# The second expert layer by pairs of experts: blocks of 128 tokens that run both experts and write finished rows

## The chip, the cores and the metric

One core of one Trainium2 chip runs the whole program. The metric is the device time in microseconds of one launch. One execution was also taken with the hardware profiler. Its rows give the traced span, and its own time stands in the table below.

## The reference

The input is 32 sequences of 256 tokens with 128 numbers each, 8192 tokens in all. Four residual blocks follow one another: a gated linear recurrence, a mixture of experts, causal attention with low-rank scores, and the same mixture of experts once more with the same weights. The change is in the last one.

```python
gate_logits = xs @ Wg                                   # 8 experts
weights, sel = jax.lax.top_k(gate_logits, 2)
weights = softmax(weights, axis=1)
h = relu(einsum('td,edf->etf', xs, W1) + b1[:, None, :])   # 128 -> 512
out_e = einsum('etf,efd->etd', h, W2) + b2[:, None, :]     # 512 -> 128
out = einsum('tk,tkd->td', weights, out_e[sel, tok[:, None]])
x = x + out                                             # xs is the layer norm of x
```

## The kernel before

`build` (L2221) calls `scan`, two setups, `ffn` for the first expert layer, `attention` and `ffn` for the second. Each is a block of its own, so the next starts when all engines are done with the last.

**Routing.** `ffn` (L871) loads x, normalises groups of four 128-token tiles (L1252 to L1275), stores the normalised rows to `normed` in DRAM, and computes the logits. VectorE then computes, one operation after another with a wait behind each (`did`, L1295), the two best experts of every token (L1310 to L1320), where each of the 16384 (token, expert) entries stands when they are sorted by expert (L1326 to L1349), and which expert each block of 256 slots belongs to (L1365). The inverse table, slot to token, comes from one-hot matrices: `onehot` (L1352) builds 2 x 128 columns and TensorE sums them (`find`, L1099), in 16 groups of 8.

**The expert loop.** There are 72 blocks (`NB`) of 256 slots, a fixed number, each with one expert. For a block GpSimd fetches 2 x 128 rows by their token number (`fetch`, L1037), TensorE turns them (`turn`), ScalarE and VectorE split them into two halves of 16 bits (`high`, `x_lo`), TensorE runs the first matrix (`up`, 12 matmuls of 256 columns), ScalarE applies bias and relu (L1223), both engines split the result (L1232 and L1410 for the high half, L1414 for the low one), TensorE runs the second matrix (`down`, 24 matmuls of 128 columns) and VectorE scales it and adds the bias (`rows`, L1417). Three terms of the split product are computed everywhere, so one product is three matmuls.

**The end.** In the first layer SyncE stores the results by slot. In the second (`by_slot` false) GpSimd scatters them, 2 x 128 rows for each block, into `picked` (`put`, L1042), three blocks behind. When all are there SyncE reads two rows back for each token and VectorE adds them with their weights to x (L1445 to L1454), and SyncE writes `out`.

The order on GpSimd's queue is fixed: fetch of block j+4 (two DMAs), then put of block j-3 (two DMAs):

```python
for j in range(NB + LAG):
    if j + AHEAD < NB:
        pool.wait_ge(xT_ps, j + 1)
        fetch(j + AHEAD)
    if j >= LAG and not by_slot:
        put(j - LAG)
```

## Time and profile before

| | us |
|---|---|
| median of 3 runs | 2487.86 (2483.36 to 2488.05) |
| the profiled execution's own time | 2479.44 |
| its traced span | 2477.7 |
| second expert layer: first load issued | 1902.0 |
| first gather of rows | 2049.7 |
| last block's result | 2424.2 |
| closing sum of the two experts | 2435.9 to 2471.7 |

Engines are PE (TensorE), PEld (its weight loads), DVE (VectorE), ACT (ScalarE), POOL (GpSimd) and SP (SyncE). A time stamp is us from the span's start. In a stretch's row the numbers are busy us, with the number of instructions in brackets, then the granted TensorE clock as a share of full speed. In a group's row stand the busy time, the mean ns of one instruction, and the idle time before it with what ended it.

### The profile page before, as it was taken

To read this page: it belongs to the slowest core of one execution; us is meant where nothing else is said; L and a number is where in the kernel's file an instruction comes from. 1 tells how busy PE (TensorE), PEld (TensorE's weight loads), DVE (VectorE), ACT (ScalarE), POOL (GpSimd) and SP (SyncE) were. 2 spreads that over 40 slices of the span, in tenths; PEclk is the share of its full clock that TensorE was granted. 3 is DMA by queue.
4 is the path that set the end of the run, shared out by engine and by line. 5 is a ranking of instruction groups with operands and counts; after the bars stand their busy time and mean duration, and the time that the engine had idled before them with its cause. 6 is when DMAs were issued, how large, how long until landed. Compare 5 with 4: busy or idle time off the path is not lost. (4 is left out here: it accounts for less than half of the span.)

```text
span 2477.7 us, 59443 instructions
## 1 busy us (share of the span) xinstructions
PE 1701.6 (69%) x16780; PEld 1378.8 (56%) x16781; DVE 1907.8 (77%) x4981; ACT 1442.7 (58%) x3723; POOL 1401.4 (57%) x1511
## 2 busy tenths in 40 slices
PE   3666575766643459995688888888885656777671
PEld 1545454443533429994477777777774625565550
DVE  5999899899946878884699889888993795445446
ACT  3666566666632238884388778777784235444440
POOL 2545445454540017773488888888874007777771
PEclk8778787777765559997799999999997558889985
DMA  1000001010024103333122111122113201111127
GB/s 27 11 16 17 23 13 26 14 26 13 22 64 124 38 9 89 90 89 57 31 54 54 49 48 53 51 53 54 48 42 86 64 0 46 50 50 50 49 50 216
DMA packets 186756, 122.01 MB, mean 49 GB/s; under 512 B 23937, under 2 KB 175393, under 8 KB 186529
## 3 DMA queue, kind: packets, MB, share of 16 engines
q1 hardware_dynamic: 149632, 69.94, 10.6%
q0 software_dynamic: 17920, 36.74, 6.1%
q10 hardware_dynamic: 18976, 12.59, 1.7%
q8 instruction: 109, 1.79, 0.3%
q14 instruction: 119, 0.97, 0.1%
HBM read 66.22 MB, written 44.04 MB: 44 GB/s over the span
## 5 line engine op out<-in xcount | busy, mean ns | idle before, releaser
L1814 POOL TENSOR_TENSOR att_pl<-att_p,att_ph 128x384 f16<-128x384 f32 x512 | 462.3, 919 | 114.8 <-ACT att_ph L2034 104.1
L1039 POOL DMA_INDIRECT ffn_xs<-normed,ffn_tokeni x288 | 305.9, 1062 | 386.9 <-DVE posi L1390 148.7
L325 POOL TENSOR_TENSOR sq<-states,qS 128x256 f32<-128x256 f32 x256 | 243.1, 949 | 332.2 <-DVE states L726 310.2
L538 ACT ACTIVATE decayed<-states,alpha 128x64 f32<-128x64 f32 x1024 | 272.2, 336 | 197.2 <-DVE states L726 195.7
L1223 ACT ACTIVATE ffn_h<-bank,b_cols 128x256 f32<-128x256 f32 x576 | 227.6, 475 | 178.5 <-PE bank L1133 176.2
L381 PE MATMUL bank<-sq,ident 128*128 128x128 f32 x1024 | 249.9, 415 | 104.2 <-POOL sq L325 104.2
L2031 ACT ACTIVATE att_p<-bank 128x384 f32<-128x384 f32 x512 | 252.4, 493 | 106.0 <-PE bank L1908 101.5
L2128 DVE TENSOR_REDUCE att_mx<-bank 128x3 f32<-128x384 f32 x512 | 277.6, 551 | 47.2 <-PE bank L1875 42.1
L381 PEld LDWEIGHTS bank<-sq,ident 128*128 128x128 f32 x1024 | 219.8, 239 | 137.2 <-POOL sq L325 111.4
L2034 ACT ACTIVATE att_ph<-bank 128x384 f16<-128x384 f32 x512 | 252.1, 492 | 0.0
L1146 PE MATMUL bank<-w_h,ffn_hh 128*128 x1152 | 231.3, 231 | 2.1 <-DVE ffn_hl L1414 1.7
L1146 PE MATMUL bank<-w_l,ffn_hh 128*128 x1152 | 229.9, 229 | 0.0
L1146 PE MATMUL bank<-w_h,ffn_hl 128*128 x1152 | 229.6, 229 | 0.0
L1414 DVE TENSOR_TENSOR ffn_hl<-ffn_h,ffn_hh 128x512 f16<-128x512 f32 x288 | 199.7, 693 | 8.5 <-ACT ffn_hh L1232 0.9
L1923 PEld LDWEIGHTS bank<-att_vx,att_ph 128*128 128x128 f16 x3072 | 179.2, 97 | 8.4 <-POOL att_pl L1814 2.0
L1874 PE MATMUL bank<-att_kp,att_qz 128*128 128x256 f16 (+1 forms) x1024 | 173.3, 252 | 12.8 <-DVE att_mx L2128 12.4
L1923 PE MATMUL bank<-att_vx,att_ph 128*128 128x9 f16 x3072 | 178.5, 168 | 1.6 <-POOL att_pl L1814 1.6
L1045 POOL DMA_INDIRECT picked<-ffn_ys,ffn_targeti x144 | 145.9, 1013 | 43.9 <-issue 40.5
L1133 PE MATMUL bank<-ffn_xh,w_h 128*128 128x256 f16 x576 | 167.5, 291 | 0.0
L1133 PE MATMUL bank<-ffn_xl,w_h 128*128 128x256 f16 x576 | 166.1, 288 | 0.0
L1133 PE MATMUL bank<-ffn_xh,w_l 128*128 128x256 f16 x576 | 165.4, 287 | 0.0
L1923 PE MATMUL bank<-att_vx,att_pl 128*128 128x9 f16 x1536 | 163.1, 167 | 0.0
(337 smaller groups left out, 5167.1 us busy)
## 6 DMA issues: line engine op xcount, KB each, us to landing
slots<-ffn_ys SPq DMA_DIRECT2D x72, 128.0 KB
ffn_x_all<-x SPq DMA_DIRECT2D x16, 512.0 KB, 7.2
normed<-ffn_xn ACTq DMA_DIRECT2D x32, 256.0 KB, 2.3
att_qz<-att_qp SPq DMA_DIRECT2D x256, 32.0 KB, 1.9
ffn_yg<-picked SPq DMA_DIRECT2D x32, 256.0 KB, 4.6
ffn_xs<-normed,ffn_tokeni POOLq DMA_INDIRECT x288
xin<-in_x SPq DMA_DIRECT2D x64, 64.0 KB, 1.9
xres<-in_x SPq DMA_DIRECT2D x64, 64.0 KB, 2.0
```

The lines of the kernel that those rows point to most:

```text
L325: nc.gpsimd.tensor_tensor(sq[:, t, :].rearrange("p (h i j) -> p h i j", h=HL, i=D), states[:, t, :].rearrange("p (h i j) -> p h i j", h=HL ...
L381: ins = nc.tensor.matmul(ps_a[:, P * n:P * n + P], ident[:, :], sv[:, :, j], start=(j == 0), stop=(j == D - 1))
L538: ins = nc.scalar.activation(decayed[:, 64 * h:64 * h + 64], states[:, (t - 1) % TC, 64 * h:64 * h + 64], ACT.Copy, scale=alpha[p][:, t, h ...
L1039: pool.indirect_dma_start(xs[j % AHEAD][:, r, :], None, A["normed"], bass.IndirectOffsetOnAxis(ap=tokeni[:, BR * j + r:BR * j + r + 1], ax ...
L1133: ins = nc.tensor.matmul(o, X.w1[w][:, bass.ds(e, 1), c, :].rearrange("p o d -> p (o d)"), x[b][:, :], start=(n == 0), stop=(n == 2))
L1146: ins = nc.tensor.matmul(ps_y[b][:, P * r:P * r + P], h[b][:, c, P * r:P * r + P], X.w2[w][:, bass.ds(e, 1), c, :].rearrange("p o d -> p ( ...
L1223: nc.scalar.activation(h32[b][:, c, :], bank[2 + 2 * b + c // 2][:, BS * (c % 2):BS * (c % 2) + BS], ACT.Relu, bias=X.b1[:, bass.ds(e, 1), c],
L1814: nc.gpsimd.tensor_tensor(pl[:, h % RP, :], p32[:, h % RP, :], ph[:, h % RP, :], ALU.subtract).then_inc(low_done, 1)
L1923: ins = mm(ps_y[p % 2][:, at_y:at_y + D + 1], pt[:, h % RP, o:o + P], vx[p][:, s, h, a, :], start=(n == 0), stop=(n == len(todo) - 1))
L2031: a(p32[:, h % RP, :], ps_st[h % 2][:, 0:SW], ACT.Exp, scale=2.0 ** (-2 * AS)).then_inc(exp_done, 1)
L2034: a(ph[:, h % RP, :], ps_st[h % 2][:, 0:SW], ACT.Exp, scale=2.0 ** (-2 * AS)).then_inc(high_done, 1)
L2128: v.tensor_reduce(mx[p % 2][:, h, :], ps_s[h % 2][:, 0:SW].rearrange("p (a n) -> p a n", n=P), AX_X, ALU.max).then_inc(max_done, 1)
```

## The change

The second layer gets a function of its own, `ffn_pairs`. A token goes by its pair of experts (28 pairs), once instead of twice. There are 96 blocks (`NBP`) of 128 slots, a fixed number. A block runs both experts of its pair on its 128 tokens, adds the two results, weighted, to the residual and scatters 128 finished rows straight into `out`. Empty slots repeat the first token of their block and write the same row again; blocks left over repeat an early block. Attention now writes its result into a table `rows` of 258 numbers (1032 bytes) for each token: the residual, the normalised row and the two weights, which SyncE stores as 8192 pieces of 8 bytes. One gather brings all three. The bias of the second matrix becomes one matmul with 3 rows for each expert; its three parts are made in the setup. In the loop ScalarE no longer takes a part of the split: VectorE makes high and low half of both experts. `fetch` runs six blocks ahead, behind `put`. Routing is done with 28 pairs instead of 8 experts, on 64 instead of 128 one-hot columns.

```diff
+        for k in range(3):
+            sp.wait_ge(split, 1 + 2 * k + 1)
+            sp.dma_start(X.b2_parts[k:k + 1, :, :].rearrange("o e d -> o (e d)"), b2_part[k][:, :]).then_inc(b2_kept, 16)
...
+        dve.wait_ge(b2_in, 32)
+        nc.vector.tensor_scalar(b2_rest[:, :], b2_rest[:, :], 2.0 ** HSPLIT, None, ALU.mult).then_inc(split, 1)
+        for k in range(3):
+            dve.wait_ge(split, 1 + 2 * k)
+            nc.vector.tensor_copy(b2_part[k][:, :], b2_rest[:, :]).then_inc(split, 1)
+            dve.wait_ge(split, 2 + 2 * k)
+            nc.vector.tensor_tensor(b2_rest[:, :], b2_rest[:, :], b2_part[k][:, :], ALU.subtract).then_inc(split, 1)
...
-def ffn(nc, ctx, A, X, ident, bank, name, src, dst, by_slot):
...
+def ffn(nc, ctx, A, X, ident, bank, name, src):
...
-            def put(j):
-                pool.wait_ge(ys_s, j + 1)
-                for r in range(BR):
-                    pool.indirect_dma_start(A["picked"], bass.IndirectOffsetOnAxis(
-                        ap=targeti[:, BR * j + r:BR * j + r + 1], axis=0),
...
-                    if k == 1:
-                        dve.wait_ge(halved, g + 1)
-                    for q in range(Q):
-                        t = Q * g + q
-                        ins = v.scalar_tensor_tensor(x_all[:, t, :], yg[g % AHEAD][:, k, q, :], w[:, t:t + 1],
-                                                     x_all[:, t, :], ALU.mult, ALU.add)
-                    ins.then_inc((halved, added)[k], 1)
...
+NP2 = NX * (NX - 1) // 2
+NBP = 96
+RW = 2 * E + 2
...
+SPARE = NBP - NT
...
+            sp.wait_ge(gates_kept, 16)
...
+            def fetch(j):
+                pool.indirect_dma_start(xs[j % (2 * AHEAD)][:, :], None, A["rows"], bass.IndirectOffsetOnAxis(
+                    ap=tokeni[:, j:j + 1], axis=0)).then_inc(fetched[j % (2 * AHEAD)], 16)
+            def put(j):
+                pool.wait_ge(ys_s, j + 1)
+                pool.indirect_dma_start(outt, bass.IndirectOffsetOnAxis(ap=tokeni[:, j:j + 1], axis=0),
+                                        ys[j % AHEAD][:, :], None).then_inc(scattered[j % AHEAD], 16)
...
+            pool.wait_ge(gates_kept, 16)
+            pool.wait_ge(route, R["token"])
+            for j in range(2 * AHEAD - 2):
+                fetch(j)
+            for j in range(2, NBP + 2):
+                put(j - 2)
+                if j + 2 * AHEAD - 4 < NBP:
+                    fetch(j + 2 * AHEAD - 4)
...
+            pe.wait_ge(route, R["mask"])
+            for k in range(NP2 // SB):
+                mk = mask[:, SB * k:SB * k + SB, :].rearrange("p e t -> p (e t)")
...
+            pe.wait_ge(route, R["id_held"])
+            nc.tensor.matmul(bank[1][:, 0:NBP], ones_all[0:1, 0:P], tid[0:1, :], start=True, stop=True).then_inc(firsts, 1)
...
+                nc.tensor.transpose(ps_x[b][:, 0:P], xs[AHEAD * half + p][:, E:2 * E], ident[:, :]).then_inc(xT_ps, 1)
...
+                    pe.wait_ge(h_relu, 2 * (j - 2) + k + 1)
+                for c in range(FC):
+                    for n, (w, x) in enumerate(((0, xh), (0, xl), (1, xh))):
+                        ins = nc.tensor.matmul(ps_h[b][k][:, P * c:P * c + P],
+                                               X.w1[w][:, bass.ds(e, 1), c, :].rearrange("p o d -> p (o d)"), x[b][:, :],
+                                               start=(n == 0), stop=(n == 2))
...
+                    pe.wait_ge(ys_s, j - 1)
+                pe.wait_ge(h_low, 2 * j + k + 1)
+                o = ps_y[b][:, P * k:P * k + P]
+                nc.tensor.matmul(o, X.ones3[0:3, :], X.b2_parts[0:3, bass.ds(e, 1), :].rearrange("p o d -> p (o d)"),
+                                 start=True, stop=False)
+                for c in range(FC):
+                    for n, (w, h) in enumerate(((0, hh), (0, hl), (1, hh))):
+                        ins = nc.tensor.matmul(o, h[b][k][:, c, :], X.w2[w][:, bass.ds(e, 1), c, :].rearrange("p o d -> p (o d)"),
+                                               start=False, stop=(c == FC - 1 and n == 2))
+                ins.then_inc(y_ps, 1)
+            load_experts(pe, regs, 0, 0)
+            turn(0, 0, 0, 0)
+            turn(0, 1, 0, 0)
...
+            def step(i, p, half, oct):
+                for k in range(2):
+                    up(i, p, k, expert(pe, regs, half, p, k))
...
+                    turn(*on_by(i, p, half, oct, 2))
+                if not (isinstance(i, int) and AHEAD * i + p < 1):
+                    ii, pp, before_half, _ = back_by(i, p, half, oct, 1)
+                    for k in range(2):
+                        down(ii, pp, k, expert(pe, regs, before_half, pp, k))
...
+                    ins = nc.scalar.activation(h32[b][k][:, c, :], bank[2 + 2 * b + k][:, P * c:P * c + P],
+                                               ACT.Relu, bias=X.b1[:, bass.ds(e, 1), c],
+                                               scale=2.0 ** (HSPLIT - SPLIT))
+                ins.then_inc(h_relu, 1)
...
+            did("lo", v.tensor_tensor(lo[:, :], i1[:, :], i2[:, :], ALU.min))
+            did("hi", v.tensor_tensor(hi[:, :], i1[:, :], i2[:, :], ALU.max))
+            did("ramp", v.tensor_scalar(ramp[:, :], lo[:, :], -0.5, NX / 2.0 - 1.5, ALU.mult, ALU.add))
+            did("start", v.scalar_tensor_tensor(start[:, :], lo[:, :], float(NX), ramp[:, :], ALU.add, ALU.mult))
+            did("pair", v.scalar_tensor_tensor(pair[:, :], hi[:, :], NX - 1.0, start[:, :], ALU.add, ALU.add))
+            did("mask", v.tensor_tensor(mask[:, :, :], pair_row[:, :].unsqueeze(2).to_broadcast([P, NP2, NT]),
+                                        pair[:, :].unsqueeze(1).to_broadcast([P, NP2, NT]), ALU.is_equal))
...
+            for k in range(NP2 // SB):
+                ins = v.tensor_copy(tot[:, SB * k:SB * k + SB, :].rearrange(flat), bank[k][:, 0:SB * NT])
...
+            did("p", v.tensor_tensor(cum[:, :, :], mask[:, :, :], base[:, :, :], ALU.mult))
+            did("pos", v.tensor_reduce(pos[:, :], cum[:, :, :].rearrange("p e t -> p t e"), AX_X, ALU.add))
...
+            did("past", v.tensor_tensor(past[:, :, :], block_row[:, :].unsqueeze(2).to_broadcast([P, NBP, NP2]),
+                                        bend[:, :].unsqueeze(1).to_broadcast([P, NBP, NP2]), ALU.is_ge))
+            did("blk", v.tensor_reduce(blk[:, :], past[:, :, :], AX_X, ALU.add))
...
+            did("twin", v.tensor_tensor(twin[:, :, :], place[:, :].unsqueeze(2).to_broadcast([P, SPARE, SPARE]),
+                                        block_row[:, 0:SPARE].unsqueeze(1).to_broadcast([P, SPARE, SPARE]), ALU.is_equal))
...
+            did("moved", v.tensor_tensor(moved[:, :, :], twin[:, :, :],
+                                         first_row[:, 0:SPARE].unsqueeze(1).to_broadcast([P, SPARE, SPARE]), ALU.mult))
+            did("moved_sum", v.tensor_reduce(more[:, :], moved[:, :, :], AX_X, ALU.add))
...
+            def h_split(i, p, k):
+                j, b = AHEAD * i + p, p % 2
+                dve.wait_ge(h_relu, 2 * j + k + 1)
+                if not early(j):
+                    dve.wait_ge(y_ps, 2 * (j - 2) + k + 1)
+                v.tensor_copy(hh[b][k][:, :, :], h32[b][k][:, :, :]).then_inc(h_high, 1)
+                dve.wait_ge(h_high, 2 * j + k + 1)
+                v.tensor_tensor(hl[b][k][:, :, :], h32[b][k][:, :, :], hh[b][k][:, :, :], ALU.subtract).then_inc(h_low, 1)
+            def rows(i, p, half):
+                j, b = AHEAD * i + p, p % 2
+                x = xs[AHEAD * half + p]
+                dve.wait_ge(y_ps, 2 * j + 2)
+                v.scalar_tensor_tensor(half_out[b][:, :], bank[6 + b][:, 0:P], x[:, 2 * E:2 * E + 1], x[:, 0:E],
+                                       ALU.mult, ALU.add).then_inc(y_half, 1)
+                dve.wait_ge(y_half, j + 1)
+                if not (isinstance(j, int) and j < AHEAD):
+                    dve.wait_ge(scattered[p], 16 * i)
+                v.scalar_tensor_tensor(ys[p][:, :], bank[6 + b][:, P:2 * P], x[:, 2 * E + 1:2 * E + 2], half_out[b][:, :],
+                                       ALU.mult, ALU.add).then_inc(ys_s, 1)
+            x_lo(0, 0)
+            x_lo(0, 1)
...
+        ffn(nc, ctx, A, experts, ident, bank, "ffn1", A["x1"])
+        attention(nc, ctx, A, heads, experts, ident, bank, A["x1"], A["x2"],
+                  A["rows"][:, 0:E].rearrange("(b t) e -> b t e", t=T))
+        ffn_pairs(nc, ctx, A, experts, ident, bank, "ffn2", A["out"])
```


## Rows read from the trace of the kernel before

**Rows 1.** Page, part 4: the chain that ended last, by line

```profile
POOL picked L1045 5%; POOL ffn_xs L1039 5%; DVE ffn_x_all L1452 1%; DMA ffn_xs<-normed,ffn_tokeni 1%; PE bank L1146 1%; PE bank L1103 1%; DVE ffn_isa L1360 1%; PE bank L1082 0%; SPq L1001 0%; ACT ffn_isa L1201 0%; DVE ffn_isb L1359 0%; DVE ffn_st L1256 0%; DVE ffn_xn L1272 0%; PE bank L1133 0%; PE bank L1073 0%
```

**Rows 2.** Stretches: first layer's loop, second layer's routing, second layer's loop

```profile
1000.00:1040.00 40.00, 40.00 (x511) 36.90 (x509) 33.11 (x68) 33.26 (x83) 31.56 (x28) 1.00 0.34 91
1980.00:2040.00 60.00, 30.75 (x118) 15.45 (x119) 56.50 (x268) 18.82 (x15) 0.00 (x0) 0.50 0.00 0
2160.00:2220.00 60.00, 45.51 (x424) 36.14 (x421) 29.65 (x59) 29.89 (x71) 46.29 (x46) 0.86 0.19 50
```

**Rows 3.** Groups of the second layer (1850 to 2478 us), GpSimd

```profile
L1039 POOL DMA_INDIRECT ffn_xs<-normed,ffn_tokeni x144 | 147.6, 1025 | 191.2 <-DVE ffn_empty L1393 147.6 <-issue 43.0 <-PE bank L1121 0.6
L1045 POOL DMA_INDIRECT picked<-ffn_ys,ffn_targeti x144 | 145.9, 1013 | 43.9 <-issue 40.5 <-DVE ffn_ys L1423 3.4
```

**Rows 4.** Groups of the first layer (690 to 1080 us), GpSimd

```profile
L1039 POOL DMA_INDIRECT ffn_xs<-normed,ffn_tokeni x115 | 128.6, 1118 | 183.5 <-DVE posi L1390 148.7 <-issue 34.2 <-PE bank L1121 0.6
```

**Rows 5.** Timeline, first layer's loop, TensorE: one block (start, us, engine, line)

```profile
1011.58 0.27 PE L1133 MATMUL bank<-ffn_xh,w_h 128*128 128x256 f16 x1
...
1012.89 0.38 PE L1121 MATMUL bank<-ident,ffn_xs 128*128 128x128 f32 x2
1013.11 0.22 PE L1146 MATMUL bank<-w_h,ffn_hh 128*128 x1
...
1014.45 0.27 PE L1133 MATMUL bank<-ffn_xh,w_h 128*128 128x256 f16 x1
```

**Rows 6.** Timeline, first layer's loop, VectorE

```profile
1012.53 0.68 DVE L1414 TENSOR_TENSOR ffn_hl<-ffn_h,ffn_hh 128x512 f16<-128x512 f32 x1
1013.13 0.42 DVE L1423 SCALAR_TENSOR_TENSOR ffn_ys<-bank,b_rows 128x256 f32<-128x256 f32 x1
1013.46 0.41 DVE L1410 CAST ffn_hh<-ffn_h 128x512 f16<-128x512 f32 x1
1013.91 0.69 DVE L1414 TENSOR_TENSOR ffn_hl<-ffn_h,ffn_hh 128x512 f16<-128x512 f32 x1
```

**Rows 7.** Timeline, first layer's loop, ScalarE

```profile
1012.54 1.57 ACT L1223 ACTIVATE ffn_h<-bank,b_cols 128x256 f32<-128x256 f32 x4 [0.39 <-PE bank L1133]
```

**Rows 8.** Timeline, first layer: the first gather and the last block's result

```profile
917.33 1.15 POOL L1039 DMA_INDIRECT ffn_xs<-normed,ffn_tokeni  x1 [148.71 <-DVE posi L1390]
...
1141.44 0.42 DVE L1423 SCALAR_TENSOR_TENSOR ffn_ys<-bank,b_rows 128x256 f32<-128x256 f32 x1 [1.20 <-PE bank L1146]
```

**Rows 9.** Timeline, second layer's routing, VectorE

```profile
1965.35 0.69 DVE L1312 TENSOR_REDUCE ffn_m<-ffn_L 128x64 f32<-128x512 f32 x1
...
1973.32 0.23 DVE L1319 TENSOR_TENSOR ffn_d<-ffn_m 128x64 f32<-128x64 f32 x1
...
1976.58 1.22 DVE L1328 TENSOR_TENSOR_SCAN ffn_cum<-onesrow,ffn_tot 128x512 f32<-128x512 f32 x1
...
1981.94 1.03 DVE L1343 TENSOR_TENSOR ffn_cand<-ffn_O,ffn_prod 128x512 f32<-128x512 f32 x1
...
1986.61 0.25 DVE L1359 TENSOR_SCALAR ffn_isb<-slot_col,ffn_col 128x128 f16<-128x128 f16 x1
```

**Rows 10.** Timeline, second layer: from the one-hot columns to the first gather

```profile
2040.45 0.75 DVE L1365 TENSOR_TENSOR ffn_past<-block_row,ffn_bend 128x576 f32<-128x576 f32 x1
...
2044.09 0.46 DVE L1375 COPY ffn_found<-bank 128x288 f32<-128x288 f32 x1 [0.79 <-PE bank L1103]
...
2049.72 0.97 POOL L1039 DMA_INDIRECT ffn_xs<-normed,ffn_tokeni  x1 [147.58 <-DVE ffn_empty L1393]
```

**Rows 11.** Timeline, second layer: the last block's result and the last stores

```profile
2423.80 0.42 DVE L1423 SCALAR_TENSOR_TENSOR ffn_ys<-bank,b_rows 128x256 f32<-128x256 f32 x1 [1.20 <-PE bank L1146]
...
2465.35 6.71 SPq L1029 DMA_DIRECT2D out<-ffn_x_all  x5
```

**Rows 12.** Timeline, start of the second layer: eight loads of 1024 pieces of 512 B

```profile
1902.00 11.06 SPq L1001 DMA_DIRECT2D ffn_x_all<-x  x8
```

**Rows 13.** Timeline, the setup's last work on VectorE

```profile
759.25 8.75 DVE L857 SCALAR_TENSOR_TENSOR w_l<-raw_w,w_h 128x4096 f16<-128x4096 f32 x2
```

512 lines of the change are left out of this document (443 added, 69 removed).

## The prediction

> **What bounds the kernel now.** I began with the chain of waits [rows 1]. Its two largest lines are GpSimd's gather (L1039) and scatter (L1045) of the second expert layer, 10% of the span together. The stretches [rows 2] show the same loop twice. In the first layer TensorE is busy 40.00 of 40 us at clock 1.00. In the second layer it is busy 45.51 of 60 us at clock 0.86, and GpSimd issues 46 indirect DMAs in 60 us, one per 1.30 us. Four belong to a block (two gathers, two scatters), so a block takes 5.2 us. The groups [rows 3] say that this is GpSimd's own pace: 1.03 and 1.01 us busy for each plus 0.3 us of issue (43.0 us over 144), and almost no wait for data (0.6 us for TensorE, 3.4 us for VectorE). So 288 DMAs at 1.30 us, 375 us, set the length of the loop. Behind it lies a serial end, in which nothing of the loop runs: from the last result at 2424.2 to the span's end at 2477.7 [rows 11]. Ahead of it lies the routing, 1965.35 to 2049.72 [rows 9, 10], where VectorE is busy 56.50 of 60 us [rows 2] with one dependent operation after the other.
>
> **Change, part 1: setup and load.** The bias of the second matrix is split on VectorE, in the setup's serial stretch, just ahead of its last work [rows 13]. That row gives 4.37 us for 4096 columns, 1.07 ns per column. For 1024 columns I take 1.2 us for each of three subtractions and 0.65 us for each of four one-source operations (a cast of 512 columns has 0.41 us, a subtraction 0.69 [rows 6]): +6.2 us, all on the path, because VectorE ends the setup. Three small DMAs run under the 8.75 us of that row. The second layer's load reads rows of 512 B at a pitch of 1032 B. Today its eight DMAs take 11.06 us to issue [rows 12] and the first statistics wait for that. Equal is 0 us; half as slow again is +5.5. I take +2. Memsets and index rows of the new function run beside this load.
>
> **Part 2: routing.** An operation of 512 columns takes 0.69 us, of 64 columns 0.23 [rows 9], and the wait for itself adds 0.035: 0.19 us plus 1.04 ns per column. Up to the first one-hot column the new list has 10 operations of 512 columns (7.2), the mask (28 x 64 = 1792 columns, 2.05), some 14 of 64 columns and a reciprocal (3.9, beside TensorE's sums), four copies out of PSUM (2.4), a scan (1.22 us for 512 columns now, so 3.8), three operations of 1792 (6.15), four sums out of PSUM (2.4), a strided reduction of 1792 (between 2.05 and twice that, as the strided 1.03 us stands to 0.69 [rows 9]; 2.7), ten small ones (2.1), and four for the column number (0.9): 33.6 us. Now it is 1986.61 - 1965.35 = 21.3. **+12.3.** One-hot columns: now 2040.45 - 1986.61 = 53.8 us for 16 groups, 3.37 each. There will be 8, each with 96 instead of 144 columns in one half, some 3.0: 24.0. **-29.8.** Then the block table (96 x 28 = 2688 columns twice, 3.0 each; 1024 columns three times, 1.26 each; 576 twice; ten small ones): 13.3 us instead of 2044.09 - 2040.45 = 3.6. **+9.7.** Then the token numbers, narrower, but with a matmul to wait for and two operations of 1024 columns: 8.9 instead of 5.6. **+3.2.** Sum of routing: -4.6, so the first gather starts at 2045.1 before the shifts of part 1. It also waits for the weights' store, issued some 20 us before the one-hot columns, so with about 66 us of cover. The load of x has as many pieces, 8192, and needs 11 us of issue [rows 12]: cost 0. If the pieces took six times as long, the wait would show. The Trainium skill (DMA: Bandwidth & Descriptors, Specifications) says that writes under 512 B are done as read-modify-write; no row here times such a store.
>
> **Part 3: the loop.** 96 blocks; the cost of one, engine by engine.
> TensorE [rows 5]: 24 matmuls of 128 columns take 1.34 us (1014.45 - 1013.11), two transposes 0.22. The new block has 48 matmuls of 128 columns (2.68), two for the bias (0.11) and one transpose (0.11): 2.9 us at clock 1.00. Twice as many matmuls now fall into twice the number of short groups with a register step; I allow up to 3.2.
> VectorE [rows 6], by the distance of starts: subtraction 0.60, cast 0.45, an operation on 256 columns 0.33, and by 1.04 ns per column 0.20 for 128. New: two casts, two subtractions, x_lo, and two row operations of which the second waits for the first (0.32): 0.9 + 1.2 + 0.2 + 0.52 = 2.8 us.
> ScalarE [rows 7]: four relus of 256 columns in 1.57 us, so 0.37 apart; for 128 columns some 0.23. Eight and the x cast: 2.4 us. Not the bound.
> GpSimd: two DMAs instead of four for a block half as large. With VectorE idle one takes 0.97 us [rows 10], in the second loop 1.03 [rows 3], in the first, where VectorE works nearly twice as densely, 1.12 on average [rows 4], and 28 in 40 us [rows 2] make 1.43 each. So two cost 2.86 us against 2 x (0.97 + 0.3) = 2.54 undisturbed: 0.32 us lost to one cast and two subtractions. The new block has two casts and two subtractions. If the casts alone do it, 3.2 us; if the subtractions do, 2.9. I take 3.1, and it sets the pace, just above TensorE. The Trainium skill (SBUF — State Buffer, Who interferes with whom) says that a cast in a two-port mode shuts GpSimd out for its whole duration, which speaks against giving VectorE more casts. By that rule the trace agrees that the DMAs get longer, and what the full rule would give is rival D.
> The first layer's loop lasts from 917.33 to 1141.86 [rows 8], 224.5 us, 16.4 more than 72 x 2.89: start at a low clock, fill and drain. The new loop: 16.4 + 96 x 3.1 = 314.0 us. Waits that are new on GpSimd's queue: the scatter of block j stands ahead of the gather of block j+6. The gather then has three block times, 9 us, to land, and a landing takes 2 to 3 us, so this hides; if the scatter is late, the next transpose is late.
>
> **Part 4: the end.** The readback, the closing sum and the stores vanish. What stays is the last result, one scatter (1.3), its landing and the release of the layer; the latter two take 2477.7 - 2472.1 = 5.6 today [rows 11]. With 0.4 for the result itself the tail is 7.3 us, of which 0.4 is already in the loop; 6.9.
>
> **The sum.** 2045.1 + 6.2 + 2 + 314.0 + 6.9 = 2374.2 against 2477.7: -103.5. Of this 2477.7 - 2424.2 = 53.5 less 6.9, so 46.6, come from the end, 4.6 from routing, 60 from the loop (374.5 from first gather to last result, now 314), and 8.2 are given back in part 1. On the profiled execution's own time, 2479.4, that is 2375.9. It lies 8.4 under the median of the runs, 2487.9; on the median it gives **2384**.
>
> **Rivals.**
> A, a gather of 1032 bytes costs GpSimd two rows' work. All gathers in the trace are of 512 B. If the time goes by bytes, a gather takes 0.97 more, a block 4.07 us, the total 93 more: 2477. That the issue is per row and not per byte is my assumption, and no row excludes the other.
> B, GpSimd is not disturbed and TensorE sets the pace at 2.9 us: 19 less, 2365. For it: TensorE at 40.00 of 40 us in the first layer [rows 2].
> D, a cast shuts out GpSimd for its length: 2.54 + 2 x 0.41 = 3.4 us, 29 more, 2413. The same comes out if TensorE's short groups cost it 0.5 us. Against: by this the first layer's two DMAs would take 2.95 us, and they take 2.86.
> E, slower: TensorE's clock. It was at 0.50 (1.2 GHz) in the routing, with TensorE busy half the time, 0.86 in the present loop and 1.00 in the first layer's [rows 2]. The new work is 2.9 us for each block at 1.00. If every block's gather comes late and the clock stays low, the loop goes as 2.9 / clock. The point at which nothing is gained is a block of 3.1 + 103.5 / 96 = 4.18 us, a clock of 0.69. At 0.5 a block takes 5.8 us, and the time is 2643. Against: TensorE would be busy over 90% of the loop, more than at 0.86 now.
> F, the change does not do what it says (blocks that wait for the weights' store, or a load far slower): within a few us of today.
>
> **How the numbers follow.** Forecast 0.45 (3.0 to 3.2 us a block, 2370 to 2400), B 0.17, D 0.22, A 0.09, E 0.05, F 0.02. The range leaves out E, F, most of A, and ends below at B with the unknowns of part 1 and 2 on the good side (12 us): 2353; above at D with 3.6 us a block, 2432, and 8 for part 1 and 2: 2440. About 0.2% is what a measurement of this kernel can tell from no change. Faster: all but E and half of F, and a sliver of A: 0.93. Same 0.02. Slower 0.05.
>
> **What would show it.** Right: 192 indirect DMAs in the second loop, one per 1.5 to 1.6 us, with hardly a wait ahead of them; last result 310 to 320 us after the first gather; TensorE above 90% busy at clock 1.00; first gather at about 2053; no work after the last scatter lands. Part 1 is wrong if the first layer starts other than 6 us later, part 2 if the one-hot groups are not near 3.0 us or the block table not near 13. The prediction is wrong at its main term if a gather of 1032 bytes takes clearly longer than the scatter beside it, if GpSimd waits for VectorE's rows (then VectorE or TensorE is the bound), or if the granted clock stays under 0.9.

## The result, and the profile after

The change makes the kernel slower: 2587.25 us (median of 4 runs, 2584.89 to 2598.25) against 2485.61 us (4 runs, 2474.41 to 2488.05), a ratio of 1.0433 with a 95% interval of 1.0406 to 1.0460. The prediction was 2384 us. The profiled execution has 2585.51 us of its own time and a span of 2583.8 us.

The chain of waits, followed back from the end of the program, has moved to another engine. Page of the changed kernel, part 4, by line; it answers to [rows 1]:

```profile
PE bank L1690 8%; PE bank L1705 7%; PE bank L1701 1%; PE bank L1679 1%; PE bank L1636 1%; DVE ffn_isa L1927 0%; SPq L1576 0%; ACT ffn_h L1782 0%; PE bank L1627 0%; DVE ffn_isb L1926 0%; DVE ffn_hl L1987 0%; DVE ffn_xn L1825 0%; DVE ffn_st L1809 0%; DVE ffn_hh L1985 0%; DVE ffn_cum L1894 0%
```

GpSimd is gone from it; what is left are TensorE's products: up (L1690), down (L1705), bias (L1701). The same three stretches as [rows 2] (length; busy time and instructions of PE, PEld, DVE, ACT, POOL; granted clock; DMA share; GB/s):

```profile
1000.00:1040.00 40.00, 40.00 (x520) 37.11 (x519) 33.14 (x68) 33.61 (x82) 31.86 (x27) 1.00 0.31 87
1980.00:2040.00 60.00, 14.08 (x71) 9.03 (x69) 58.59 (x176) 7.47 (x8) 0.00 (x0) 0.53 0.19 1
2160.00:2220.00 60.00, 52.10 (x541) 36.21 (x539) 32.24 (x74) 26.64 (x99) 21.51 (x22) 0.94 0.13 37
```

In the second layer's loop GpSimd issues 22 DMAs in 60 us, not the 38 of my forecast. TensorE is busy 52.10 of 60 us at clock 0.94 (1.00 is its level of 2.4 GHz), and no other engine is busy for more than 32.24 us. Where the loop begins (timeline, GpSimd):

```profile
2048.62 0.97 POOL L1599 DMA_INDIRECT ffn_xs<-token_rows,ffn_tokeni  x1 [142.46 <-DVE ffn_tokeni L1973]
```

The line of the scatter, with what GpSimd waited for ahead of it (ns min/median/max; first and last start; us, times):

```profile
L1604 POOL DMA_INDIRECT out<-ffn_ys,ffn_tokeni x96: 967/985/1003, 2062.1 to 2572.1; - x96
...
  DVE ffn_ys L1999: 306.7, 96
```

The line that writes the rows:

```profile
L1999 DVE SCALAR_TENSOR_TENSOR ffn_ys<-bank,ffn_xs,ffn_half_out x96: 349/351/353, 2061.5 to 2571.5; 128x128 f32<-128x128 f32 x96
```

The first gather starts at 2048.62, 4.4 us ahead of the 2053 that I had. From the first to the last block's rows it is 2571.5 - 2061.5 = 510.0 us, 5.37 us a block, where I had 3.1. So what I am off by, some 200 us, lies in the loop. GpSimd, which was to set the pace, stands for 306.7 us and waits for VectorE's rows.

Inside a block, TensorE at clock 1.00 (timeline; start and length in us):

```profile
2112.22 0.23 PE L1690 MATMUL bank<-ffn_xh,w_h 128*128 128x128 f16 x1
2112.29 0.22 PE L1690 MATMUL bank<-ffn_xl,w_h 128*128 128x128 f16 x1
2112.34 0.22 PE L1690 MATMUL bank<-ffn_xh,w_l 128*128 128x128 f16 x1
2112.46 0.23 PE L1690 MATMUL bank<-ffn_xh,w_h 128*128 128x128 f16 x1
...
2112.70 0.23 PE L1690 MATMUL bank<-ffn_xh,w_h 128*128 128x128 f16 x1
...
2112.93 0.23 PE L1690 MATMUL bank<-ffn_xh,w_h 128*128 128x128 f16 x1
```

By the work of an engine's queue I mean the instructions in its rows that are neither matmuls nor weight loads: register steps, reads of registers, waits, branches. What TensorE's queue does at the same line (count; ns min/median/max; first and last start):

```profile
L1690 PEldq ALU_OP  x768: 32/32/36, 2053.0 to 2565.5; - x192
...
L1690 PEldq FUSED_REGOPS  x766: 46/46/52, 2052.9 to 2565.4; - x192
```

Groups of three matmuls start 0.24 us apart (2112.22, .46, .70, .93). Three matmuls of 128 columns on this engine take 0.167 us (24 in 1.34 us, [rows 5]). The 0.07 us more are about what two register instructions last that TensorE's queue has for each group: 46 ns and 32 ns, 8 of each per block here and 8 more at L1705. They work out the address of the weights from the expert's number; a group has one such pair. The Trainium skill (Perfetto Trace Analysis, Sequencer Loop) has the sequencer read the next instruction, push it into a queue if it is one for the engine, and start executing it itself if it is a control instruction. If that is so, such a step is hidden only while the engine has work queued, which experiments 1, 2 and 5 bear out.

And every 16 blocks the engine stands (timeline, TensorE; in brackets the idle time ahead):

```profile
2178.71 0.29 PE L1690 MATMUL bank<-ffn_xh,w_h 128*128 128x128 f16 x1 [3.84 <-issue]
```

The same at 2266.67, 2354.57 and 2443.61. Ahead of each stands the branch that closes the loop's body (TensorE's queue; the last of the five does not turn):

```profile
L1532 PEldq COMPARE_BRANCH  x5: 83/3467/3552, 2174.8 to 2527.8; - x5
```

Theory 1: the address steps cost the time; they are exposed because a group now has half the columns to hide them behind. Theory 2: short groups, or the round of waits between the engines, cost it whatever the addresses. Theory 3: the bias products cost it. Beside these stand the turns of the loop.

The experiments were spread over six chips. Four of them take 2587 to 2602 us for the kernel before (B below), two take 2481 (A), so totals of B are not set against those of A. Where nothing else is said I compare the second layer's loop, from the first to the last block's rows (L1999 or the line that writes them), and ratios are to the kernel before on the same chip.

| run | chip | total us | ratio to before, interval | loop us |
|---|---|---|---|---|
| changed (three times) | A | 2587.3, 2588.6, 2584.3 | 1.043, 1.043, 1.042 | 510.0, 511.3, 509.9 |
| constants, all | B, B, A | 2486.0, 2483.5, 2410.6 | 0.961, 0.955, 0.972 (0.969 to 0.975) | 360.7, 358.9, 332.9 |
| constants, up only | B | 2505.7 | 0.969 | 382.1 |
| no bias | B | 2605.0 | 1.007 | 485.0 |
| body of 8 blocks | B, B, B | 2607.0, 2608.7, 2609.5 | 1.008, 1.003, 1.003 | 484.1, 486.2, 486.1 |
| wide down | A | 2503.2 | 1.0095 (1.0079 to 1.0112) | 415.9 |
| wide down, body of 8 | B, A | 2529.2, 2481.3 | 0.974, 1.0002 (0.9987 to 1.0017) | 395.8, 395.2 |
| the same, read moved | B | 2530.1 | 0.973 (0.971 to 0.974) | 395.7 |
| blocks of 256 | B | 2608.8 | 1.0037 (1.0019 to 1.0055) | 473.0 |

### The profile page after: what moved, and what is told of

Same layout as the page of the kernel before. It is cut to its first block and busy times, and to the rows that moved or that the text cites. A ratio compares the mean times of both kernels' runs of the same rounds, so it can differ in the third digit from the quotient of the medians.

```text
span 2583.8 us, 66961 instructions
## 1 busy us (share of the span) xinstructions
PE 1871.8 (72%) x18884; PEld 1477.1 (57%) x18885; DVE 1985.7 (77%) x5072; ACT 1476.7 (57%) x4147; POOL 1293.4 (50%) x1424
## 5 line engine op out<-in xcount | busy, mean ns | idle before, releaser
L1782 ACT ACTIVATE ffn_h<-bank,b_cols 128x128 f32<-128x128 f32 x768 | 213.8, 368 | 283.0 <-PE bank L1690 281.7
L1030 POOL DMA_INDIRECT ffn_xs<-normed,ffn_tokeni x144 | 154.0, 1069 | 199.8 <-DVE posi L1368 148.8
L1604 POOL DMA_INDIRECT out<-ffn_ys,ffn_tokeni x96 | 94.6, 985 | 306.7 <-DVE ffn_ys L1999 306.7
L1985 DVE CAST ffn_hh<-ffn_h 128x512 f16<-128x512 f32 x192 | 81.2, 423 | 180.8 <-ACT ffn_h L1782 180.5
L1690 PE MATMUL bank<-ffn_xh,w_h 128*128 128x128 f16 x768 | 180.5, 235 | 26.0 <-issue 16.9
L1599 POOL DMA_INDIRECT ffn_xs<-token_rows,ffn_tokeni x96 | 94.1, 980 | 171.5 <-DVE ffn_tokeni L1973 142.5
L1690 PE MATMUL bank<-ffn_xl,w_h 128*128 128x128 f16 x768 | 174.8, 228 | 0.0
L1690 PE MATMUL bank<-ffn_xh,w_l 128*128 128x128 f16 x768 | 174.4, 228 | 0.0
L1705 PE MATMUL bank<-w_h,ffn_hh 128*128 x768 | 172.5, 230 | 0.4
L1705 PE MATMUL bank<-w_l,ffn_hh 128*128 x768 | 167.3, 221 | 0.0
L1705 PE MATMUL bank<-w_h,ffn_hl 128*128 x768 | 167.2, 222 | 0.0
```

Of the source, the lines that this page charges most:

```text
L1690: ins = nc.tensor.matmul(ps_h[b][k][:, P * c:P * c + P], X.w1[w][:, bass.ds(e, 1), c, :].rearrange("p o d -> p (o d)"), x[b][:, :], start= ...
L1705: ins = nc.tensor.matmul(o, h[b][k][:, c, :], X.w2[w][:, bass.ds(e, 1), c, :].rearrange("p o d -> p (o d)"), start=False, stop=(c == FC - ...
L1782: ins = nc.scalar.activation(h32[b][k][:, c, :], bank[2 + 2 * b + k][:, P * c:P * c + P], ACT.Relu, bias=X.b1[:, bass.ds(e, 1), c], scale= ...
```

## Experiments

**1. Constant experts on TensorE.** For `up`, `down` and bias:

```diff
-    X.w1[w][:, bass.ds(e, 1), c, :]
+    X.w1[w][:, k:k + 1, c, :]
```

> Left out: the choice of experts on TensorE. In the second layer's loop every block multiplies by experts 0 and 1 (constants in the program) instead of the two of its pair; the number, shape and order of matmuls, waits, transfers and the work of ScalarE, VectorE and GpSimd stay. Theory 1 (the address steps): in the changed kernel a group of three 128-column matmuls starts every 0.236 us where 0.167 us were expected, and two register steps of 46 and 32 ns stand before each group on TensorE's queue. With constants the steps are gone: groups every 0.16 to 0.17 us, a block in 2.9 to 3.3 us instead of 5.0 to 5.4 us (GpSimd's 2 x 0.98 us and VectorE's 2.8 us allow it), the whole in 2365 to 2400 us. Theory 2 (short matmuls: a 128-column group costs 0.236 us whatever its addresses, or the loop is held by the round of waits between the engines): the steps lie beside other work, the time stays within 10 us of the changed kernel's 2587 us. Theory 3 (the bias product and the change of experts): only what stands at those places goes, 2540 to 2560 us.

> The kernel with constant experts once more (experts 0 and 1 in place of the pair's on TensorE in the second layer), because the chip of the first call took 2587 us for the kernel before the change, 4 per cent more than the others, and there the total of this one cannot be set against 2587 us of the changed kernel. Theory 1: the second layer's loop takes 345 to 361 us instead of 511 us, the whole 2425 to 2440 us (TensorE's block is 3.3 us at the full clock by its timeline, not the 2.9 us of my forecast: the bias products take 0.2 us with their gaps each). Had the first call's chip been what made the difference: 2587 us.

> Constant experts on TensorE in the second layer (0 and 1 in place of the block's pair). Its loop took 361 and 359 us on the two slow chips against 511 us of the changed kernel on the fast ones. If the kind of chip has no part in that, the loop is 355 to 365 us on a fast chip too and the whole 2587 - 150 = 2437 us, a ratio of 0.98 to the kernel before; if it has, 2480 us.

On the chip that ran the changed kernel in 2584.3 us this one takes 2410.6: 173.7 us less, 177 of them in the loop. No register instruction is left at the three lines, and in the third run the matmuls run through at 0.055 us (timeline, TensorE, third of the three runs):

```profile
2220.47 0.22 PE L1690 MATMUL bank<-ffn_xh,w_h 128*128 128x128 f16 x1
2220.52 0.22 PE L1690 MATMUL bank<-ffn_xl,w_h 128*128 128x128 f16 x1
2220.58 0.22 PE L1690 MATMUL bank<-ffn_xh,w_l 128*128 128x128 f16 x1
2220.63 0.28 PE L1679 MATMUL bank<-ident,ffn_xs 128*128 128x128 f32 x1
2220.84 0.22 PE L1701 MATMUL bank<-b_parts,ones 3*128 3x128 f16 x1
2221.00 0.23 PE L1705 MATMUL bank<-w_h,ffn_hh 128*128 128x128 f16 x1
```

Its line of the rows, and then a stretch of its loop (columns as above):

```profile
L1999 DVE SCALAR_TENSOR_TENSOR ffn_ys<-bank,ffn_xs,ffn_half_out x96: 349/351/352, 2062.6 to 2395.5; 128x128 f32<-128x128 f32 x96
```

```profile
2170.00:2230.00 60.00, 57.30 (x857) 51.02 (x857) 50.58 (x119) 39.32 (x151) 35.29 (x34) 0.97 0.21 58
```

857 matmuls in 60 us instead of 541, with the same tiles and the same waits between engines, and 3.50 us a block. Theory 2 falls: the fewer columns of a matmul are not what is slow.

The edit takes away more than the address steps. With constants nothing on TensorE uses the expert numbers, and the queue's reads of them are gone from this trace too, though the source still has them. In the changed kernel they are:

```profile
L1548 PEldq TENSOR_LOAD <-ffn_blki x24: 588/606/725, 2047.3 to 2540.1; - x24
```

Summed over the loop, the queue's own instructions (register steps, reads, waits, branches) last 183.6 us in the changed kernel and 36.9 us in the third run. That is 147 of the 177 us; the other 30 no row tells apart. So the experiment shows the price of the queue's work for chosen experts, of which the address steps are the largest part.

The first two runs, on B, have a loop of 360.7 and 358.9 us: on those chips this kernel's loop is slower too. A loop that TensorE's queue holds more tightly does not show that (395.2 and 395.8 us, experiment 6).

**2. Constants for the up products only.**

```diff
-    up(i, p, k, expert(pe, regs, half, p, k))
+    up(i, p, k, None)    # expert k
```

> Left out: the choice of experts in the first matrix's products alone (the second layer's up products use experts 0 and 1; down and its bias still use the pair of the block). Theory 1 says the cost is per group that has a new register address, and half of them are left: 8 of 16 groups of a block are freed of 0.07 to 0.08 us each, with the start of an expert some 0.15 us more, so 0.6 to 0.9 us a block of 96, 60 to 90 us: 2497 to 2530 us. Theory 2: no change, 2577 to 2597 us. If all the cost were in the down products and the bias, 2577 to 2597 us as well, with the first experiment at 2370 to 2400 us.

The loop takes 382.1 us, beside 360.7 with all constant on the same chip. The changed kernel did not run there; set against its 510 us on A, half of the steps gone takes away more than half of the cost. Here the down products still have their steps, and can run at full pace in spite of them (line of the down products in TensorE's queue, then timeline):

```profile
L1705 PEldq FUSED_REGOPS  x768: 46/46/52, 2100.6 to 2486.6; - x192
L1705 PEldq ALU_OP  x768: 32/32/36, 2100.7 to 2486.7; - x192
```

```profile
2255.31 0.22 PE L1705 MATMUL bank<-w_h,ffn_hl 128*128 x1
2255.36 0.22 PE L1705 MATMUL bank<-w_l,ffn_hh 128*128 x1
2255.43 0.23 PE L1705 MATMUL bank<-w_h,ffn_hh 128*128 x1
```

In this stretch the step that costs 0.07 us in the changed kernel costs 0.01 us. It is not so everywhere: over the loop (2150 to 2480 us) the down groups start 0.18 us apart in the median, a third of them 0.225 us or more. In the changed kernel it is 0.24 us in the median and three quarters, with all constant 0.17 us and 2%. So the step does not have one price. The reading that fits is that the queue gets ahead in the up products, and the steps of the down products cost nothing until that lead is used up. In the changed kernel no part of the block gives it a lead.

**3. No bias products.**

```diff
-    nc.tensor.matmul(o, X.ones3[0:3, :], X.b2_parts[0:3, bass.ds(e, 1), :]..., start=True, stop=False)
...
-    start=False
+    start=(c == 0 and n == 0)
```

> Left out: the second matrix's bias (the product of ones with b2 that opens each down sum in the second layer); all else stays, with addresses in registers. Theory 3: the two bias products of a block with the gaps around them take 0.3 us each, so 0.6 us a block, 58 us: 2530 us. Theory 1: a bias product has one register step (46 ns) and 0.06 us of matmul, twice a block: 0.2 us a block, 20 us: 2567 us.

The loop is 485.0 us. The body has 16 blocks, as in the changed kernel, which did not run on a chip B, so I set it against 510 with reserve: 25 us, 0.26 a block. That is near the 0.2 of theory 1 and half of what theory 3 has. The stands at the turns are longer there (4.0 to 5.1 us instead of 3.8), so the bias products can be a little dearer than that, but they are no main term.

**4. A loop body of 8 blocks instead of 16.**

```diff
-    LOOPS = (NQD - 4) // BODY
+    LOOPS = (NQD - 4) // PBODY    # 2; the body's range and indices follow
```

> Nothing is left out: the loop over the second layer's blocks is unrolled by 8 blocks instead of 16, so it turns back 9 times instead of 4. In the changed kernel TensorE stands for 3.9 to 4.0 us at each of four places 16 blocks apart, for nothing that the profile shows. If this is the price of each turn (reading the body anew), there are 5 more of it: 5 x 3.9 = 20 us more, 2607 us. If it goes with the length of the body, each turn costs half, 9 x 2 = 18 us against 4 x 3.9 = 16 us: 2587 to 2590 us. If a body that is short enough stays at hand, the turns cost nothing: 2571 us.

> The changed kernel with a loop body of 8 blocks once more, on another chip than the first time. Its loop took 484 us there against 510 us; if that was the body, the four stands of 3.9 us and smaller ones are gone here too: 2587 - 26 = 2561 us. If it was the chip: 2585 to 2610 us.

> The changed kernel with a loop body of 8 blocks instead of 16, hoping for a fast chip. Its trace on the slow chips has no stand at the turns and the loop took 484 and 486 us, against 510 us on the fast ones with a body of 16: 2587 - 26 = 2561 us, 1.031 of the kernel before, on a fast chip; on a slow one 1.003 to 1.008 as before.

Three runs, all on B: loops of 484.1, 486.2 and 486.1 us, 25 us under the changed kernel's on A, as hoped; 9 turns, and at none of them a stand of TensorE. Branch of the loop in the third run, TensorE's queue:

```profile
L1533 PEldq COMPARE_BRANCH  x10: 76/208/223, 2183.0 to 2553.1; - x10
```

The branch lasts 0.21 us instead of 3.5. What fetches instructions shows why. DMA queues in 350 us of the loop (packets, MB, share), the changed kernel first, then the third run with the body of 8:

```profile
q8 instruction: 44, 0.72, 0.8%
q14 instruction: 23, 0.19, 0.2%
```

```profile
q8 instruction: 4, 0.07, 0.1%
q14 instruction: 3, 0.02, 0.0%
```

The body of 16 is fetched anew in each of the four passes, 11 packets of 16 KB on q8 for one, spread over its 88 us; the body of 8 is not. The first expert layer's body has 16 blocks too, of 38 instead of 51 matmuls each; it turns without a stand of 0.3 us or more in the changed kernel's trace (940 to 1140 us). My first guess, a price for each turn, was wrong. That the total does not show the 25 us against the kernel before (1.003 to 1.008) is B's doing: see 9. With the wide down products of 5, the two bodies are compared on A in 6.

**5. Wide down products.** The two halves of w2 lie side by side, and the high part of h is multiplied by both at once:

```diff
+    nc.tensor.matmul(both, hh[b][k][:, c, :], w2m[:, bass.ds(e, 1), c, :, :]...)      # 256 columns
+    nc.tensor.matmul(o, hl[b][k][:, c, :], w2m[:, bass.ds(e, 1), c, 0, :]...)         # 128 columns
...
-    for n, (w, h) in enumerate(((0, hh), (0, hl), (1, hh))):    # three of 128
```

VectorE adds four sums with the residual instead of two. The bias product, which opened each sum, now stands behind the first group.

> Nothing is left out. In the second layer's down products the two halves of w2 lie side by side (copied once by two transfers before the loop), and the high part of h is multiplied by both in one matmul of 256 columns, the low part by the first half in one of 128: two matmuls and one address a group instead of three and two, the same columns. VectorE adds the two sums with two more operations a block of 0.35 us (2.8 to 3.5 us a block, beside TensorE's 5). Theory 1 (TensorE's queue is the bound: register steps of 46 and 32 ns and 0.054 us for each weight load with its matmul): 8 groups a block lose one 32 ns step and one pair of 0.054 us each, 0.69 us a block, 66 us in 96 blocks: 2520 us. Theory 2 (columns and waits are the bound; the columns stay 384 a group): no change or 10 to 30 us slower by the longer end of a block, 2587 to 2617 us.

2503.2 us, 1.0095 of the kernel before: 85 us less than the changed kernel on the same chip and 95 us less in the loop (415.9 us), 19 to 29 more than the 66 of theory 1. The columns are the same and VectorE does more. Timeline, TensorE, from the down products into the next block's up products:

```profile
2303.08 0.27 PE L1715 MATMUL bank<-ffn_w2m,ffn_hh 128*128 x1
2303.19 0.22 PE L1720 MATMUL bank<-ffn_w2m,ffn_hl 128*128 x1
2303.24 0.27 PE L1715 MATMUL bank<-ffn_w2m,ffn_hh 128*128 x1
2303.35 0.22 PE L1702 MATMUL bank<-ffn_xh,w_h 128*128 128x128 f16 x1
...
2303.52 0.22 PE L1702 MATMUL bank<-ffn_xh,w_h 128*128 128x128 f16 x1
...
2303.76 0.23 PE L1702 MATMUL bank<-ffn_xh,w_h 128*128 128x128 f16 x1
...
2303.99 0.23 PE L1702 MATMUL bank<-ffn_xh,w_h 128*128 128x128 f16 x1
...
2304.32 0.23 PE L1702 MATMUL bank<-ffn_xh,w_h 128*128 128x128 f16 x1
```

A down group now takes 0.16 us, its columns' time. The first two up groups behind it start 0.17 us apart, the next ones 0.24 and more: the lead won in the down products is spent within the up products. This is one reason why it gained more than its own steps. Another can be the moved bias product: from the matmul ahead of it to the one behind it pass 0.31 us in the median instead of 0.46, twice a block. The two were not taken apart.

**6. Wide down products and a body of 8 blocks.**

> The wide down products (2503 us, with TensorE standing 3.2 to 3.8 us at each of the four turns of the loop) with a loop body of 8 blocks instead of 16. If a body of 8 blocks turns for nothing, as its trace in the narrow form showed no such stand: 2503 - 13.6 = 2488 to 2490 us. If each turn costs the same whatever the body: 5 more turns of 3.4 us, 2520 us.

> Wide down products and a loop body of 8 blocks. On a fast chip: 2503 us less the four stands of 3.2 to 3.8 us at the turns, 2488 to 2492 us, a ratio of 1.003 to 1.005 to the kernel before. On a slow chip as measured there, 2525 to 2535 us, a ratio of 0.974.

The loop takes 395.2 us on A and 395.8 on B, 20.7 less than with the body of 16. Its four stands of 3.2 to 3.8 us were 13.6 of that. On A 2481.3 us, 1.0002 of the kernel before (0.9987 to 1.0017); on B 0.974.

**7. The expert numbers read behind the down products.** In that kernel TensorE stands at each read of the next four blocks' experts:

```profile
2256.18 0.22 PE L1703 MATMUL bank<-ffn_xh,w_l 128*128 128x128 f16 x1
2257.16 0.32 PE L1692 MATMUL bank<-ident,ffn_x_all 128*128 128x128 f32 x1 [0.77 <-issue]
```

```diff
     for k in range(2):
         up(i, p, k, expert(pe, regs, half, p, k))
-    if p == AHEAD - 2 and within(i, 0, AHEAD):
-        load_experts(pe, regs, 1 - half, i + 1)
...
         down(ii, pp, k, expert(pe, regs, before_half, pp, k))
+    if p == AHEAD - 2 and within(i, 0, AHEAD):
+        load_experts(pe, regs, 1 - half, i + 1)
```

> Nothing is left out: wide down products, a loop body of 8 blocks, and TensorE's read of the next four blocks' expert numbers moved from behind the up products to behind the down products. In the last kernel TensorE stands 0.55 to 0.78 us at each of these reads, in every fourth block, 24 times, where its queue has just used up its lead on the up products; behind the down products the queue is ahead. If the stand is covered there: 24 x 0.7 = 17 us less, 2465 us and 0.993 of the kernel before on a fast chip (0.967 on a slow one, where it was 0.974 without). If the read costs its time wherever it stands: no change, 1.000 (0.974).

It missed the 17 us hoped for, and that says much. The stands are gone (none over 0.4 us that waits for nothing in 2200 to 2400), and the loop is 395.7 us against 395.8: nothing is won. This fits a queue that is the bound and pays for each of its instructions wherever it stands; the 0.7 us had only been where the lead ran out.

**8. Blocks of 256 tokens.** 60 blocks, up products of 256 columns, down products in two halves that share their addresses.

```diff
-NBP = 96
+NBP = 60
+NTL = NBP * BR      # tiles of 128 slots
```

> Nothing is left out: the same idea (tokens grouped by their pair, both experts in a block, finished rows) with blocks of 256 tokens, 60 of them instead of 96 of 128, so each weight address serves 256 columns in the first matrix and two halves of the block in the second (register steps a row fall to half, and lie beside 0.33 us of matmul as in the first layer's loop, rows 5); TensorE 2 x (1.31 + 1.34) + 0.22 us and four bias products of about 0.11 us, 5.9 us a block; VectorE 5.4 us, ScalarE 4.9 us, GpSimd 4 x 0.98 = 3.9 us. Theory 1: the loop is 60 x 5.9 + 16 = 370 us instead of 527 us, the whole 2430 to 2450 us, faster than both kernels (ratio to the kernel before 0.98 to 0.99). Theory 2 (waits and the count of blocks with little overlap are the bound, not the address steps): VectorE's 5.4 us on a block with 5.9 us of TensorE leaves more waits, 6.6 to 7 us a block, 2475 to 2500 us.

2608.8 us on B, 1.0037, and not the gain of either theory. The loop takes 473.0 / 59 = 8.0 us a block, not 5.9. Two parts of it can be read. From the matmul ahead of a bias product to the one behind it pass 0.3 us, four times a block, where I had 0.11. And in most blocks TensorE loses time among matmuls of one group, 0.9 us a block in the mean of 2150 to 2560 us; one block (timeline, TensorE):

```profile
2251.89 0.22 PE L1723 MATMUL bank<-w_h,ffn_hh 128*128 x1
2252.51 0.22 PE L1723 MATMUL bank<-w_h,ffn_hl 128*128 x1 [0.40 <-issue]
2253.25 0.22 PE L1723 MATMUL bank<-w_l,ffn_hh 128*128 x1 [0.53 <-issue]
```

Nothing that the profile shows is waited for there. It is no fetch of the body as in 4, since the instruction queues moved 13 packets in 350 us. What it is stays open, and so does the rest of the 2.1 us. That larger blocks pay off is not shown.

**9. The changed kernel and the kernel before, again.**

> The changed kernel itself, once more. In the four kernels of the first call the FIRST expert layer, which none of them alters, took some 35 us longer from its first to its last block (945 to 1188 us on the constants kernel, 937.6 to 1146.4 us in the changed kernel's trace), so that what they gained in the second layer shows only in part in their totals. If this is a state that the first layer falls into whatever the kernel, it shows here too, with the total still near 2587 us and so the second layer's loop nearer 470 us than 510 us. If it comes from the edits, the first layer takes 209 us here and the second 510 us.

> The kernel before the change, once more, beside the changed kernel: 2486 us, a ratio of 0.96 to the changed kernel. Its first expert layer took 224.5 us from first gather to last rows; 35 us more there would show that the longer first layer belongs to the state of the run and not to the edits, 224 to 226 us that it does not show in this kernel.

> The changed kernel, third time, beside the kernel before. Two of the three chips so far ran the kernel before in 2587 and 2600 us, one in 2481. On a chip of the slow kind I expect its first layer at 238 us instead of 209 us and its second layer's loop at 505 to 515 us, since the second loop is held by TensorE's queue and not by the rhythm between the engines: 2587 + 30 + 15 = 2620 to 2640 us, a ratio to the kernel before of 1.01 to 1.02, so that most of the loss of 4.3 per cent would be hidden by what the kernel before loses there. On a chip of the fast kind: 2587 us, 1.043.

> The kernel before, for its trace on the same chip. On a slow chip: both expert layers' loops turn in 3.3 to 3.4 us a block instead of 2.9 to 3.0 us, 2 x 72 x 0.45 = 65 us, which is most of its 100 us more. On a fast chip: 2481 us and the rows already read.

> The kernel before once more, for its trace on a chip where it takes 2600 us, if this is one. There: the first layer's loop in 3.3 us a block (238 us from its first to its last rows against 209 us), the stretch up to the second layer's statistics 44 us later than 1915 us as in the other kernels' traces on such chips, and the remaining 70 us in the second layer's loop, which waits for its gathers (72 x 1 us). On a fast chip it shows 2481 us and nothing new.

The first four ran on A and repeat the result: 1.0434 (1.0413 to 1.0455) and 1.0418 (1.0388 to 1.0447). The last ran on B: 2585.1 us. Its first layer goes from first to last rows in 235.4 us instead of 208.9, its second layer from first gather to last rows in 443.2 us instead of 380.8, and 14 us more lie between. What VectorE waits for ahead of the rows that GpSimd scatters, kernel before on B:

```profile
L1423 DVE SCALAR_TENSOR_TENSOR ffn_ys<-bank,b_rows x144: 409/417/426, 939.0 to 2537.1; 128x256 f32<-128x256 f32 x144
its engine sat idle before it (us, times) until:
  remote: 117.1, 30
```

These are waits, most of them of 3 to 6 us and 117 us in all, that the profile puts down to no engine of the core. On A the same line waits 10.0 us, 18 times, for the scatter's landing (`DMA picked<-ffn_ys`), and has no `remote`. The issue of a gather is not slower on B (second layer: 989 ns median against 990 on A). That the waits are the landings of its scatters fits the code (each of four result buffers is written again when its scatter has landed, and the scatter is issued three blocks behind), but was not tested. The name alone proves nothing: ScalarE's relus (L1223), which wait for engines only, have 181.1 us of `remote` there too (2120 to 2500 us). The changed kernel itself was not run on a chip B.

## Why the prediction was wrong

**What held.** Part 1: the first layer's statistics start 5.1 us later (784.84 for 779.71) where I had 6.2 for the split of the bias. Part 2: the first one-hot column comes 33.7 us into the routing (33.6 predicted), a group takes 3.02 us (3.0), the first gather starts at 2048.6 (2053). The weights' store of 8192 pieces of 8 bytes kept the DMA engines busy for 8 us (1982.6 to 1990.9), under the cover named. GpSimd's gather of 1032 bytes has a median of 970 ns and the scatter 985: rival A, twice the price, is refuted by its own mark. So is rival D's first form for this loop: the casts are doubled in the block, and the DMAs got no longer. By the rule of the Trainium skill (SBUF — State Buffer, Who interferes with whom) a cast in a two-port mode should lengthen them where the two meet; no row tells the mode of these casts, in this loop GpSimd works for only 21.51 of 60 us, so they can seldom meet, and the trace neither shows nor excludes it. Where VectorE is busier they can be longer: in the third run of experiment 1 (50.58 of 60 us) the gather's median is 1.05 us and the scatter's 1.13, in the first, on B (about 47 of 60 us), 0.98 and 0.99. The clock stood at 0.91 to 1.00 in the loop, so rival E is refuted as well: the kernel is slower, and for another reason than the one I had priced.

**What failed.** One term: "TensorE ... 2.9 us at clock 1.00. Twice as many matmuls now fall into twice the number of short groups with a register step; I allow up to 3.2." I saw the step and priced it at up to 0.3 us a block. What the queue does for chosen experts costs 1.9: with constant experts a block takes 3.50 us, with the experts of its pair 5.37. So TensorE's queue sets the pace of the loop, and not GpSimd, which my sum had just above it. Most of it can be worked out from rows that the trace of before had. There a group of three matmuls of 256 columns lasts 0.33 us [rows 5], and two steps of 0.078 us together lie beside it. The down products' 24 short matmuls ran in 1.34 us because the second half of a block took the addresses of the first, and, as experiment 2 suggests, because the queue came to them with a lead from the up products. Where it came without one, the same trace shows the price. Second layer, kernel before, TensorE behind a wait for a gather (timeline; four down groups with new addresses, then one that uses an address again):

```profile
2162.47 0.43 PE L1121 MATMUL bank<-ident,ffn_xs 128*128 128x128 f32 x2 [1.86 <-DMA ffn_xs<-normed,ffn_tokeni]
2162.78 0.23 PE L1146 MATMUL bank<-w_h,ffn_hh 128*128 x1
...
2163.03 0.23 PE L1146 MATMUL bank<-w_h,ffn_hh 128*128 x1
...
2163.37 0.23 PE L1146 MATMUL bank<-w_h,ffn_hh 128*128 x1
...
2163.60 0.23 PE L1146 MATMUL bank<-w_h,ffn_hh 128*128 x1
...
2163.78 0.24 PE L1146 MATMUL bank<-w_h,ffn_hh 128*128 x1
```

The groups start 0.25, 0.34 and 0.23 us apart, and the first that uses an address again follows after 0.18. The new block has 16 groups of 0.167 us, each with a step of 0.078 and nothing to get ahead with: 16 x (0.167 + 0.078) = 3.9 us, and with two bias products with their own steps and the gaps behind them (0.3 each), the transpose (0.3) and the read of the experts (0.7 in four blocks), 5.0. The rows of two blocks start 5.06 us apart in the median, and with a body of 8 blocks a block takes 5.1 in the mean. I took durations from groups whose cost was hidden and carried them to groups that hide nothing.

**A smaller miss.** The turns of the loop: 25 us (experiments 4 and 6). The body has as many blocks as the one of before, but no longer stays at hand between turns. And the tail: from the start of the last result to the span's end 12.3 us (2571.5 to 2583.8), where I had 7.3.

**The sum, after the fact.** From the first gather to the end of the last result I had 314 us; it took 523.2 (2048.6 to 2571.8), 209 more. Of these, 177 go with constant experts (experiment 1), 147 of them the queue's own instructions. The 32 left are the 3.50 us a block of the constants kernel over my 3.1, which make 38, less 6 for a shorter start. In the 3.50 are four turns (stands of 11 us) and the gaps around bias product and transpose: my 2.9 us for TensorE were low even without a step, the median block there takes 3.33. The change did save what it was to save: the readback and the closing sum, and GpSimd as the bound. With the queue relieved (experiment 6) it comes to the kernel before on A, and 2.6% under it on B; no version here that computes the whole result is faster on A by more than the interval.

**The range.** It ended at 2440, 147 us short. Rival D named the right engine as its second form, "TensorE's short groups cost it 0.5 us", at a quarter of the size. The point at which nothing is gained, 4.18 us a block, held: experiment 6 has 4.16 and comes out even. In part this is luck, since a tail 5 us too long and a start 6 us too short cancel in that sum.

## What to carry to other kernels

An engine has two times to add up, that of its work and that of its queue. A timeline of the work shows the second only where it is not hidden; the queue's own rows show it always. When tiles are made smaller, count what the queue does for each group (address steps, waits, reads of registers) beside the columns that it has to hide behind, and take the price from its rows even if it costs nothing today. Where the queue is the bound, fewer instructions help, as wider matmuls did here; moving one did not. And before a loop with a longer body is judged, look at the branch that closes it and at the instruction queues, which show whether it is fetched anew in each pass.

## What the runs showed that I had not expected

- Register steps on TensorE's queue, 46 and 32 ns, cost 0.07 us a group at 128 columns and next to nothing where the queue is ahead (experiments 1, 2 and 5).
- In the changed kernel's loop the queue's own instructions last 183.6 us. With 0.167 us for three of its 4802 matmuls (267 us in all) that makes 451 of the 510 us: the two times all but add up. In the wide kernel with a body of 8 they are 147.2 and the same 267 us, 415 against a loop of 395.2, so there a part is hidden.
- A loop body of 16 of these blocks is fetched anew in each pass, with a branch of 3.5 us and a stand of 3.8 us on TensorE; one of 8 is not (44 against 4 packets of 16 KB in 350 us, a branch of 0.21 us).
- Chips differ by 4 to 5% for the kernel before (2481 and 2587 to 2602 us), and by nothing for the second loop of the wide kernel with a body of 8 (395.2 and 395.8 us). The first layer's loop falls into another rhythm there: TensorE waits for VectorE's halves, GpSimd for TensorE, 3.3 us a block instead of 2.9. Why some chips do this was not found. A version judged on one chip alone (0.974 on B) would have been taken for a gain.
